# Moving a row of 128 running minima into its place: TensorE transpose and cast, or a GpSimd DMA per row

## The reference, cut to what matters

```python
qk = jnp.einsum('bhqid,bhkjd->bhqkij', qr, kr)
qk_max = jax.lax.stop_gradient(qk.max(axis=-1, keepdims=True))
exp_qk = jnp.exp(qk - qk_max)
...
num = (attn * renorm[..., None]).sum(axis=3)
den = (exp_sum * renorm).sum(axis=3)[..., None]
out = num / (1e-08 + den)
```

## Time and profile before

| | |
|---|---|
| median of 2 runs | 8166.73 us (8162.94 to 8170.51) |
| the profiled execution | 8159.8 us, span of its slowest core 8158.2 us |
| spans of the 8 cores in it | 8129.2 to 8158.2 us |
| TensorE busy, VectorE, ScalarE, GpSimd | 74%, 32%, 20%, 8% of the span |
| projections for Q and first layer norms | up to about 400 us |
| attention, 8 pairs of heads | about 400 to 5160 us |
| output projection, feed-forward net | about 5160 us to the end |

### The profile page before, as it was taken

How to read it: one execution, slowest core, us unless ns; L and a number is a source line. 1 busy time by engine, 2 the same in 40 slices (tenths; PEclk the granted TensorE clock), 3 DMA queues, 4 the chain that set the end, 5 groups by cost and what they waited for, 6 DMA issues and landing times.

```text
span 8158.2 us, 80999 instructions; the slowest of 8 cores (8129.2 to 8158.2 us)
## 1 busy us (share of the span) xinstructions
PE 6048.9 (74%) x21776; PEld 2125.8 (26%) x21776; DVE 2632.5 (32%) x4391; ACT 1602.3 (20%) x1826; POOL 642.6 (8%) x737
## 2 busy tenths in 40 slices
PE   2457767767767767767667677548999988999995
PEld 0121121121211211211211211213444433444442
DVE  6444344344344344344344344542100012000002
ACT  0212312312312312212222222213010102210100
POOL 0000000000000000000000000001222221122222
PEclk6765565565655655655755755869999999999998
DMA  3000000000000000000000000146778897677777
GB/s 43 13 4 1 1 4 1 1 4 1 1 4 1 3 1 1 4 1 1 4 1 1 1 1 11 52 89 77 75 76 78 78 88 113 71 76 78 78 78 98
DMA packets 783662, 267.63 MB, mean 33 GB/s; under 512 B 684520, under 2 KB 760688, under 8 KB 783216
## 3 DMA queue, kind: packets, MB, share of 16 engines
q0 software_dynamic: 759408, 218.18, 26.5%
q1 hardware_dynamic: 23808, 44.27, 1.7%
HBM read 461.67 MB, written 16.78 MB: 59 GB/s over the span
## 4 chain that ended last, share of the span: by engine, by line
PE 68%; DVE 18%; issue 7%; DMA 4%; ACT 2%; DVEq 1%; POOL 0%; ACTq 0%; POOLq 0%; SPq 0%
PE psST L862 22%; PE psST L647 9%; DVE PF L598 9%; PE psP1a L592 6%; PE psPVa L633 6%; PE psP1b L592 6%; PE psPVb L633 4%; PE psST L806 3%; PE psST L813 3%; PE psST L525 2%; PE psST L890 2%; DMA PB<-w3t 2%; ACT PB L657 2%; DVE PF L664 1%; PE psST L547 1%
## 5 line engine op out<-in xcount | busy, mean ns | idle before, releaser
L862 PE MATMUL psST<-PB 128*128 128x512 bf16 x8192 | 1771.8, 379 | 18.0 <-DMA PB<-h1t 18.0
L657 ACT ACTIVATE PB<-psST 128x1024 bf16<-128x1024 f32 x1024 | 1041.3, 1024 | 3225.4 <-PE psST L647 3220.7
L862 PEld LDWEIGHTS psST<-PB 128*128 128x128 bf16 x8192 | 802.2, 98 | 987.3 <-issue 23.2
L598 DVE TENSOR_REDUCE PF<-psP1a 128x1 f32<-128x512 f32 x1024 | 708.2, 692 | 969.4 <-PE psP1a L592 941.9
L592 PE MATMUL psP1a<-PB 64*128 64x512 bf16 x1024 | 615.0, 601 | 520.2 <-DVE PF L598 431.9
L647 PE MATMUL psST<-PB 65*128 65x512 bf16 x2048 | 979.7, 577 | 19.5 <-DVE PB L616 19.5
L598 DVE TENSOR_REDUCE PF<-psP1b 128x1 f32<-128x512 f32 x1024 | 708.2, 692 | 866.8 <-PE psP1b L592 823.6
L592 PE MATMUL psP1b<-PB 64*128 64x512 bf16 x1024 | 620.5, 606 | 382.2 <-DVE PF L598 382.2
L401 DVE CAST PB<-PF 128x512 bf16<-128x512 f32 x128 | 55.9, 437 | 2208.3 <-ACT PF L896 2051.5
L633 PE MATMUL psPVa<-PB 128*65 128x512 bf16 x1024 | 591.4, 578 | 48.9 <-ACT PB L657 46.1
L633 PE MATMUL psPVb<-PB 128*65 128x512 bf16 x1024 | 588.6, 575 | 0.0
(11 more groups left out here) (115 smaller groups left out, 3547.8 us busy)
## 6 DMA issues: line engine op xcount, KB each, us to landing
PB<-h1t POOLq DMA_DIRECT2D x256, 256.0 KB, 5.9
PB<-h2t POOLq DMA_DIRECT2D x256, 256.0 KB, 5.8
PB<-w3t POOLq DMA_DIRECT2D x128, 256.0 KB, 6.8
PB<-w1t POOLq DMA_DIRECT2D x32, 512.0 KB, 8.9
PB<-w2t POOLq DMA_DIRECT2D x32, 512.0 KB, 9.6
PF<-x1d SPq DMA_DIRECT2D x8, 2048.0 KB, 14.1
PB<-xT POOLq DMA_DIRECT2D x8, 1024.0 KB, 11.9
PF<-xT SPq DMA_DIRECT2D x4, 2048.0 KB, 9.7
```

The costliest lines, as they stand in the source:

```text
L598: p.op("vector", lambda v: v.reduce_max(PF.view(col, 1), pa[:, :], axis=AX.X, negate=True), reads=[pb], writes=[b_cm[gsl], b_big1], tag="s ...
L657: p.op("scalar", lambda s, par=par, pst=pst: s.activation(PB.t[:, o_pt + par * 1024:o_pt + (par + 1) * 1024], pst[:, :], AF.Exp), reads=bs ...
L862: p.op("tensor", lambda t, j=j, sb=sb, ps=ps, wi=wi, src=src: t.matmul(ps, PB.view(o_ws + wi * 4096 + j * 128, 128), src[j][:, sb * 512:(s ...
```

## The change

`th2` no longer goes through TensorE and PSUM. The minimum of each head goes to a column of its own (`col = gc0 + qs * 2 + h`), and a DMA on the GpSimd queue reads that column (128 partitions, one fp32 number each) and writes it as 128 bf16 numbers into row 64 of the query tile. The DMAs of a query block share one semaphore, `sem_gg[gsl]`. They read `b_gc[gsl]` and write `b_qgg[gsl]`. The list of steps has as many entries as before.

```diff
+        sem_gg = [p.dma_sem("gg0"), p.dma_sem("gg1")]
...
                     for h in range(2):
-                        p.op("vector", lambda v, h=h: v.tensor_reduce(
-                            PF.view(gc0 + 64, 1), PF.view(base + h * 8, NSEG),
+                        col = gc0 + qs * 2 + h
+                        p.op("vector", lambda v, h=h, col=col: v.tensor_reduce(
+                            PF.view(col, 1), PF.view(base + h * 8, NSEG),
                             axis=AX.X, op=ALU.min),
                             reads=[b_cm[gsl]], writes=[b_gc[gsl], b_big1], tag="gmin")
-                        pt_ = psP1a if h == 0 else psP1b
-                        bpt_ = bP1a if h == 0 else bP1b
-                        p.op("tensor", lambda t, pt_=pt_: t.transpose(
-                            pt_[0:65, 0:128], PF.view(gc0, 65), idm_t[:, :]),
-                            reads=[b_gc[gsl], bidm], writes=[bpt_], tag="gT")
-                        p.op("vector", lambda v, h=h, pt_=pt_: v.tensor_copy(
+                        p.dma("gpsimd", lambda g, h=h, col=col: g.dma_start(
                             PB.t[64:65, o_qg + (gsl * 2 + h) * 512 + qs * 128:
                                  o_qg + (gsl * 2 + h) * 512 + qs * 128 + 128],
-                            pt_[64:65, 0:128]),
-                            reads=[bpt_], writes=[b_qgg[gsl]], tag="gcp")
+                            PF.t[0:128, col:col + 1]),
+                            sem_gg[gsl], reads=[b_gc[gsl]], writes=[b_qgg[gsl]],
+                            tag="grow")
```

## The result

The changed kernel is slower: 8473.8 us (median of 11 runs) against 8253.7 us for the kernel before (10 runs taken beside it), ratio 1.033 with a 95% interval of 1.026 to 1.039. The prediction had 8260 us with a range up to 8440, that is a ratio of 1.012. The shortest executions took 8162.9 us before and 8425.6 us after.

The account below looks back on a forecast made before the run. TensorE's own order was taken to set the end, with whatever it waits for in a `th2` delaying everything. 160 landings at L = 3.08 us less 393 us gave +100 on 8159.8, so 8260 us, range 8145 to 8440.

Parts of the forecast that it names:

- 160 L - 393: Attention stage: summed change over all 128 `th2`, 160 landings paid against 393 us of removed work; +100 us.
- L: Time from the end of a minimum to the start of what waits for its DMA: 0.57 + 2.4 + 0.11 = 3.08 us.
- Two DMAs in a row at the end of a pass, one wait inside, the chain onto TensorE: Ends of 32 passes: both DMAs bare, 2L - 2.22 each; inside, the second minimum waits, delaying reductions and TensorE.
- Standing alone: 24 `th2` in the pass 1 that stands alone: next bank already filled, change L - 2.21 us each.
- first in their pop: 24 `th2` at step 34 of interleaved passes, first of two steps popped together: change L - 3.35 us each.
- From the start of the DMA to landing: Landing of each new DMA: taken as 2.4 us, between a 128-number row at 1.7 and `ones_b` at 2.5 or 3.3.
- the rival of the slow landing: New DMAs land as slowly as `ones_b` on core 2 or slower: 8404 us at 3.3, 8532 at 4.1; chance 0.32.
- From VectorE's end to the start of a waiting DMA on POOL: Delay between a minimum's end and its DMA's start on GpSimd: 0.57 us, the first of three parts of L.
- The minimum of head 1 writes `b_gc[gsl]`: In each `th2`, VectorE's second minimum waits until head 0's DMA has landed, though columns differ: 128 waits of L.
- This pairing stays: Steps popped in twos: matmuls on different banks give a `kc` of 2.82 us, same bank waits for VectorE; unchanged.
- Costs nothing: `wk`, `wv` behind the 32 DMAs: Next pair's weight loads queue behind this pair's DMAs but fit in VectorE's idle 41.05 us; uncovered, 66 us in all.
- The clock: Rival: TensorE reaches its upper clock where pass 1 runs inside pass 2, 460 us less, 7700 to 7800 us; chance 0.02.

Follow-up runs that it names:

- e5: e1 with the DMA reading 128 neighbouring numbers of one partition, the maxima left out of the scores; ratio to the kernel before 0.992.
- e1: The changed kernel with each new DMA waiting once per semaphore, for the highest count, instead of once per earlier reader; ratio to the kernel before 1.0155.
- e2: The changed kernel with a name of its own for each column of minima; ratio to the kernel before 1.039, attention stage 4921.3 us.
- e7: e2 with a semaphore for each head's DMAs instead of one for both; ratio to the kernel before 0.985, attention stage 4566.5 us.
- e8: e4 with each `th2` called in the step of its group's last reduction, 65 steps instead of 69; ratio to the kernel before 0.934.
- e4: e3 with the transposes and casts of the kernel before in each pass's last group; stage 4447.2 us, ratio 0.973 when run again.
- e3: e1, e2 and e7 joined, plus a name for each head's row 64; ratio to the kernel before 0.975, attention stage 4488.2 us.
- e6: e3 with minima written as bf16 and the DMAs on the SP queue without cast; ratio to the kernel before 0.974, stage 4473.7 us.

## Why the prediction was wrong

The forecast was 8260 us, within 2%; the kernel is 3.3% slower. The counts and the four formulas held; one term was mis-sized, three were missing, and one of these decides. By parts, for the attention stage of core 5:

| term | forecast | after, worked out from the rows |
|---|---|---|
| 160 L - 393 | L = 3.08, +100 us | L = 3.48, +164 us |
| 64 fulfilled waits ahead of the first DMA of 30 passes | not seen | 30 x 4.0 = +120 us |
| the queries' SP copy starts ahead of the wait | not seen | about -33 us |
| one more wait instruction ahead of each first minimum | not seen | 126 x 0.07 = +9 us |
| sum | +100 us | +260 us, measured +263 |

- **Two DMAs in a row at the end of a pass, one wait inside, the chain onto TensorE:** right. 128 waits of VectorE, 32 of TensorE; the end of a pass takes 7.3 us against 2L + 0.32 = 7.28; the pair of `kc` 8.65 against 8.66. Standing alone, from the first minimum to the next reduction, it is 3.93 us at the median against L + 0.43 = 3.91; first in their pop two `kc` take 6.81 us against 6.59 before, 0.22 more where L - 3.35 gives 0.13.
- **"From the start of the DMA to landing", "I take 2.4":** mis-sized. It measures 2.8, the start behind the minimum 0.60 instead of 0.57, so L = 3.48 and 64 us more. The likeliest case was given as "above 2.0 and below 2.8"; the result stands at its edge, where the rival of the slow landing began. Of the two rows between which 2.4 was put, `ones_b` was the nearer, at 2.5 us against 1.7: e5 shows that collecting from 128 partitions is what counts (2.8 us, and 1.5 for one row of as many bytes), and both were measured long after the start-up. The Trainium skill, "DMA: Bandwidth & Descriptors", gives a fixed cost of about 2.0 us for such a DMA (section "Anatomy of one DMA — SWDGE (gpsimd) path"), and one descriptor per element where the last dimension is not contiguous (section "Rules for kernel authors"). The traces show 1.5 and 2.8 us, on either side of the 2.0. The rule on elements points the way that e5 measured, and I cited it without pricing it.
- **"From VectorE's end to the start of a waiting DMA on POOL: 5350.38 - 5349.81 = 0.57 us", taken for all 256:** the step that failed outright. It holds for 226 of them (0.60 us at the median) and for the first DMA of 30 passes it is 4.5 to 4.9 us. I named what the new waits wait for and took a fulfilled wait to cost nothing. The text even told how a reader's dependence arises, and I did not ask how many readers there are: 64, on an engine that had no earlier wait to cover them. e1 shows 118 us. This term brought the ratio from 1.016 (e1) to 1.033; the landing alone leaves it within the 2% of the forecast.
- **The range up to 8440:** its upper end was drawn for another reason, a landing of 3.5 us. The stage's 263 us on the forecast's base of 8159.8 give 8423 us, and the shortest execution, 8425.6, lies below 8440 as well; the median of 8473.8 does not. That the increase itself would still have fitted is luck: no path in the prediction leads to it. The base does not hold for the medians either: beside the changed kernel the kernel before has 8253.7 us, 87 us above the median of the two runs known at the forecast.
- **"The minimum of head 1 writes `b_gc[gsl]`":** right but not the whole cause, as e2 against e7 shows.
- **"This pairing stays":** right, and the reading of the slow `kc` behind it is what e8 bears out.
- **Costs nothing: `wk`, `wv` behind the 32 DMAs:** right; the seven K and V projections inside the stage take 402 us before and 401 after, and no K or V matmul waits for a weight load.
- **The early copy.** VectorE gets to the next pass's copy of queries (L580) while the last DMA is in flight, so that the SP copy has landed when the first pass-1 matmul needs it. That matmul's waits fell from 64.0 us in 32 places to 30.9 in 8. e4 is the nearest to a test of it: with the transposes back at the ends of the passes the wait is back in all 32, 72.9 us in total. The DMAs before them differ too, so that it is not a test of the copy alone.
- **The clock:** no change in the changed kernel, as said; the stretches with pass 1 inside pass 2 stay at a granted 0.50.

## What to carry to other kernels

When work moves to another engine, count the instructions that its dependences become there, not only whether they are fulfilled: with a helper like this one, an engine that has not yet waited for a semaphore is given one wait for each rising count, and here they ran after the wait that matters. A DMA in place of a short round trip through TensorE pays only where nothing queued behind it waits; here it was worth 2.7% once its false waits (a shared name, a shared semaphore, a list of readers) were gone and its bare places had their transposes back. If a wait on a DMA is written as a wait for all that was issued on its semaphore, a shared semaphore makes it a wait for the youngest of them.

A gap between two dependent instructions has to be read up to the last one that waits: the first score matmul made two DMAs in flight look 1.0 us cheaper than they were (1.29 us over the kernel before, where the second one shows 2.26).

## What the runs showed of the hardware

- A fulfilled wait costs GpSimd 61 ns, of which the record shows 17 ns as the instruction. 63 of them are 3.8 us; without them the stage is 118 us shorter in 30 places, 3.9 us each.
- A DMA of 128 single numbers from 128 partitions into one lands after 2.8 us, of one row of 128 numbers after 1.5 us; both on the GpSimd queue with a cast to bf16. With two of the first kind in flight, started some 0.6 us apart, the first lands after 2.8 us and the second after 3.7 on GpSimd (e3), after 2.8 and 3.6 on SP without the cast (e6).
- From the end of a VectorE instruction to the start of a DMA that waits for it: 0.6 us on GpSimd, 0.13 us on SP.
